# Query phase of a cross-attention kernel: four PSUM banks, one-instruction aggregates for the moments, the first two products split by term, and a new order of work on ScalarE and VectorE

## The chip, the cores and the metric

The kernel runs on one core of a Trainium2 chip. The number that counts is the device time of one execution in microseconds. The kernel before took 1082.04 us (median of 3 runs, 1081.27 to 1082.4). A core has TensorE (PE in the rows), VectorE (DVE), ScalarE (ACT), GpSimd (POOL) and SyncE (SP), which here issues all the DMAs. Each engine works through its own list of instructions in order; semaphores tie the lists together.

## The reference

```
x  : 32 x 100 x 256     ctx : 32 x 361 x 256     16 heads of 64
x  = x + xattn(layernorm(x), ctx, ctx, WQ, WK, WV, WO, mask)
x  = x + ffn(layernorm(x), W1, b1, W2, b2)

xattn: Qh = Q WQ, Kh = K WK, Vh = V WV, softmax(Qh Kh^T / 8 - 1e9 mask) Vh, heads side by side, times WO
ffn:   activations and weights rounded to 8 bits (one scale per tensor), 256 -> 1024, gelu, 1024 -> 256
```

Here mask has the shape 100 x 361 and everything is float32.

## The kernel before

Float32 products are made out of float16 ones. An operand is split into a high float16 part and a low one (the rest), and `split3` adds up three matmuls: high x high, high x low, low x high. In the rows these are lines L368, L369 and L370.

The program has four stages.

1. The query phase, 0 to 98 us. It normalises x and multiplies it by WQ for all 32 batches, while the four attention weights are scaled and split.
2. The turns of the batches. For each batch, K, V, the scores, the softmax, the product with V and the product with WO follow a table of times that gives each engine its order. The table is not changed.
3. The feed-forward network.
4. The output.

The query phase goes in eight chunks of four batches, 400 tokens each. A chunk c takes these steps:

- `stats_x` (VectorE, BN_STATS, one instruction a batch) gives the moments of the even and the odd elements. `ln_moments` joins them in eight small dependent steps, for chunk 0 on VectorE and for the others on GpSimd; GpSimd then makes `rstd` and `shift`.
- `norm_x` (ScalarE, four instructions) writes the normalised `xn`. `x_transposes` (TensorE, eight) brings it into two PSUM banks. `x_high` (ScalarE, two) and `x_low` (VectorE, two) split it into `xnT_h` and `xnT_l`.
- In `q_chunk` TensorE makes eight products m = 0 to 7, each with six matmuls of 400 columns (two halves of the contraction, three terms). They go in turn into PSUM banks `proj[0]` and `proj[1]`. `q_out` copies each product out: ScalarE the even ones, VectorE the odd ones. The semaphores `s_qe` keep product m from starting before product m-2 has been copied. At m = 4 TensorE does the transposes of chunk c+1.

The weights take part in between. `abs_w` (VectorE, two per weight) finds the largest value in each partition, `top_w` (TensorE) transposes it, and `unit_w` (VectorE, three small steps) makes the scale. `high_w` (ScalarE) and `low_w` (VectorE) then write the two parts, half a weight at a time. No product of queries can start before WQ has been through this.

After the last chunk `phase1_over` makes every engine wait for all query outputs. TensorE also waits for GpSimd's memsets (`s_zero`) there, and then begins with the K products, which use the same two banks as the query products.

## Time and profile before

| | us |
|---|---|
| median of 3 runs | 1082.04 |
| the profiled execution | 1081.73 |
| its span | 1079.9 |
| query phase, first to last product | 20.07 to 97.9 |
| PE busy | 1019.1 (94%) |
| DVE busy | 937.4 (87%) |
| ACT busy | 862.5 (80%) |
| POOL busy | 766.1 (71%) |

The span is the time from the first to the last instruction on the core, and 1.8 us of the execution lie around it. In the rows below, a line number such as L368 is the line of the kernel that issued the instruction. Matmuls are pipelined, so one matmul's duration overlaps the next; what a matmul costs in a stream is the distance between two starts. `x4` at the end of a row counts instructions that were merged. `[0.79 <-issue]` is idle time before the instruction and what ended it.

### The profile page before, as it was taken

To read this page: it belongs to the slowest core of one execution; us is meant where nothing else is said; L and a number is where in the kernel's file an instruction comes from. 1 tells how busy PE (TensorE), PEld (TensorE's weight loads), DVE (VectorE), ACT (ScalarE), POOL (GpSimd) and SP (SyncE) were. 2 spreads that over 40 slices of the span, in tenths; PEclk is the share of its full clock that TensorE was granted. 3 is DMA by queue.
4 is the path that set the end of the run, shared out by engine and by line. 5 is a ranking of instruction groups with operands and counts; after the bars stand their busy time and mean duration, and the time that the engine had idled before them with its cause. 6 is when DMAs were issued, how large, how long until landed. Compare 5 with 4: busy or idle time off the path is not lost.

```text
span 1079.9 us, 37623 instructions
## 1 busy us (share of the span) xinstructions
PE 1019.1 (94%) x10639; PEld 650.5 (60%) x10639; DVE 937.4 (87%) x2668; ACT 862.5 (80%) x1809; POOL 766.1 (71%) x1106
## 2 busy tenths in 40 slices
PE   3999999999999999999999999999999999997738
PEld 1555566666666666666666666666666666665327
DVE  5776888888898888888888888888888888886997
ACT  3664888888888888888888888888888888886906
POOL 3336778877777887777887778777777777774700
PEclk9999999999999999999999999999999999999969
DMA  8500676666767676666667767666766666673003
GB/s 238 142 1 14 122 141 139 138 138 138 138 138 140 140 140 139 138 138 138 138 139 140 140 136 138 140 138 139 138 138 139 133 137 140 138 144 127 1 0 123
DMA packets 435437, 136.77 MB, mean 127 GB/s; under 512 B 407666, under 2 KB 434390, under 8 KB 435414
## 3 DMA queue, kind: packets, MB, share of 16 engines
q1 hardware_dynamic: 435414, 136.47, 61.1%
q8 instruction: 13, 0.21, 0.1%
q14 instruction: 10, 0.08, 0.0%
HBM read 28.60 MB, written 6.55 MB: 33 GB/s over the span
## 4 chain that ended last, share of the span: by engine, by line
PE 88%; DVE 7%; ACT 2%; issue 1%; DMA 1%; POOL 0%; ACTq 0%; DVEq 0%; SPq 0%; POOLq 0%
PE front L368 21%; PE front L369 19%; PE front L370 19%; PE back L1309 13%; PE front L1287 7%; PE tp L1287 5%; DVE hrange L1138 3%; DVE hrange L1139 3%; DMA xs<-x 1%; PE front L1424 1%; ACT xn L691 1%; PE tp L1424 1%; PE back L1424 0%; PE front L1192 0%; PE front L1213 0%
## 5 line engine op out<-in xcount | busy, mean ns | idle before, releaser
L616 POOL TENSOR_TENSOR hl<-prob,hl 100x361 f16<-100x361 f32 x511 | 428.6, 853 | 74.6 <-ACT hl L748 73.8
L742 ACT ACTIVATE prob<-prob,nmax 100x361 f32<-100x361 f32 x512 | 295.4, 589 | 5.0 <-DVE nmax L985 3.7
L1309 PEld LDWEIGHTS back<-v,pT 128*128 128x128 f16 (+1 forms) x4608 | 167.8, 98 | 32.3 <-issue 9.6
L748 ACT ACTIVATE hl<-prob 100x361 f16<-100x361 f32 x352 | 175.2, 498 | 3.4
L1309 PE MATMUL back<-v,pT 128*128 128x65 f16 (+1 forms) x4608 | 176.9, 193 | 0.8 <-DMA pT<-hl 0.8
L752 ACT ACTIVATE k_h<-front 128x362 f16<-128x362 f32 x256 | 120.5, 471 | 61.8 <-PE front L370 54.2
L368 PE MATMUL front<-ctx_h,wk_h 128*128 128x362 f16 x512 | 164.0, 320 | 2.4 <-DVE v L1045 1.0
L370 PE MATMUL front<-ctx_h,wk_l 128*128 128x362 f16 x512 | 161.7, 316 | 0.0
L369 PE MATMUL front<-ctx_l,wk_h 128*128 128x362 f16 x512 | 161.4, 315 | 0.0
L1045 DVE SCALAR_TENSOR_TENSOR v<-front,v 128x512 f16<-128x512 f32 (+1 forms) x192 | 132.6, 691 | 30.6 <-ACT v L756 29.9
L756 ACT ACTIVATE v<-front 128x512 f16<-128x512 f32 (+1 forms) x192 | 114.4, 596 | 55.4 <-PE front L370 49.8
L985 DVE CUSTOM_DVE_ANT_0 prob<-tp,mask_g,ngain 100x361 f32<-100x361 f32 x256 | 148.2, 588 | 11.0 <-POOL hl L616 7.6
L985 DVE CUSTOM_DVE_ANT_0 prob<-front,mask_g,ngain 100x361 f32<-100x361 f32 x256 | 148.5, 589 | 5.7 <-POOL hl L616 0.3
L368 PE MATMUL front<-wv_h,ctx_h 128*128 128x512 f16 (+1 forms) x384 | 147.6, 384 | 1.7 <-DVE k_l L1039 1.2
L369 PE MATMUL front<-wv_l,ctx_h 128*128 128x512 f16 (+1 forms) x384 | 145.5, 379 | 0.0
L370 PE MATMUL front<-wv_h,ctx_l 128*128 128x512 f16 (+1 forms) x384 | 145.5, 379 | 0.0
L1039 DVE SCALAR_TENSOR_TENSOR k_l<-front,k_h 128x362 f16<-128x362 f32 x256 | 135.6, 530 | 7.0 <-ACT k_h L752 3.7
L620 POOL TENSOR_TENSOR ahl<-att,ahl 100x256 f16<-100x256 f32 x127 | 85.1, 670 | 36.8 <-ACT ahl L762 36.8
L605 POOL TENSOR_TENSOR ctx_l<-ctx_raw,ctx_h 128x361 f16<-128x361 f32 x64 | 53.2, 854 | 44.3 <-ACT ctx_h L792 44.3
L992 DVE TENSOR_SCALAR_CACHE_REDUCE hl<-prob 100x361 f16<-100x361 f32 x160 | 83.8, 524 | 0.7 <-ACT prob L742 0.6
L368 PEld LDWEIGHTS front<-ctx_h,wk_h 128*128 128x128 f16 x512 | 49.7, 97 | 47.4 <-issue 10.7
L368 PEld LDWEIGHTS front<-wv_h,ctx_h 128*128 128x128 f16 (+1 forms) x384 | 41.1, 107 | 59.2 <-issue 19.1
(206 smaller groups left out, 2047.4 us busy)
## 6 DMA issues: line engine op xcount, KB each, us to landing
ctx_raw<-ctxT SPq DMA_DIRECT2D x33, 361.0 KB, 3.2
pT<-hl SPq DMA_TRANSPOSE x253, 3.6
xs<-x SPq DMA_DIRECT2D x8, 400.0 KB
q_all<-x SPq DMA_DIRECT2D x32, 100.0 KB
out<-q_all SPq DMA_DIRECT2D x32, 100.0 KB
xb<-out SPq DMA_DIRECT2D x5, 640.0 KB, 8.2
out<-xb SPq DMA_DIRECT2D x25, 128.0 KB, 1.8
q_all<-wq SPq DMA_DIRECT2D x1, 1024.0 KB, 6.8
```

Of the source, the lines that this page charges most:

```text
L368: eng.matmul(dst, lh, rh, start=first, stop=False)
L369: eng.matmul(dst, lh, rl, start=False, stop=False)
L370: return eng.matmul(dst, ll, rh, start=False, stop=final)
L616: pool.tensor_tensor(hl[0:T, n % RT, 1, 0:S], prob[0:T, n % RP, 0:S], hl[0:T, n % RT, 0, 0:S], ALU.subtract).then_inc(s_lo, 1)
L742: act.activation(prob[0:T, n % RP, 0:S], prob[0:T, n % RP, 0:S], ACT.Exp, bias=nmax[0:T, n:n + 1], scale=-1.0).then_inc(s_exp, 1)
L748: act.activation(hl[0:T, h % RT, 0, 0:S], prob[0:T, h % RP, 0:S], ACT.Copy).then_inc(s_ha, 1)
L752: act.activation(k_h[:, n % 4, :], ps[:, 0:SE], ACT.Copy, scale=KS).then_inc(s_kh, 1)
L985: dve.tensor_tensor_reduce(prob[0:T, n % RP, 0:S], ring[n % RP][0:T, 0:S], mask_g[0:T, 0:S], ngain[0:T, 0:1], 3.0e38, ALU.add, ALU.min, nm ...
L1039: dve.scalar_tensor_tensor(out=k_l[:, n % 4, :], in0=ps[:, 0:SE], scalar=KS, in1=k_h[:, n % 4, :], op0=ALU.mult, op1=ALU.subtract).then_in ...
L1045: dve.scalar_tensor_tensor(out=v[:, 1], in0=ps[0:rows_of(n), :].rearrange("p (h d) -> p h d", h=HT), scalar=VS, in1=v[:, 0], op0=ALU.mult, ...
L1287: ins = pe.matmul(ring[(2 * n + h) % RP][:, 0:SE], qs[rows[h], n, :], ks[rows[h], n % 4, :], start=t == 0, stop=t == 2)
L1309: ins = pe.matmul(obank[j % 2][:, n % GH * DV:(n % GH + 1) * DV], pT[0:r, n % RT, part_ * ST + st, :], v2[half][0:r, st, v, n % HT, :], st ...
```

## The change

It touches the query phase and the first waits behind it.

- Query products use four banks in turn, `qbank = proj + obank`. Product m waits for the copy of product m-4. ScalarE still takes the even products and VectorE the odd ones.
- TensorE runs small matmuls on the identity from the start: `warm_up(120)` gives 240 matmuls of 64 x 100, half of them into PSUM partitions 0 to 63 and half into 64 to 127. After that come `top_w(0)` and then `x_transposes(0, 0)`, in the other order than before, and 56 more such matmuls.
- `first_two` makes products 0 and 1 of chunk 0 term by term: first all high x high matmuls, then those with `xnT_l`, then those with `wq_l`. The first half of WQ is split in two quarters, so products 0 and 1 need only the first quarter.
- For chunks 0 and 1 the moments come from BN_AGGR, one for each batch, in `pair_x` on VectorE. Two small steps make `var` and `mean` from its output.
- VectorE looks for the maxima of WQ ahead of the statistics of chunk 1, of which one batch goes before `unit_w(0)` and three behind it.
- On ScalarE `norm_x` of a chunk is done in two halves, ahead of and behind `q_out(6)`. The second `high_w` of a chunk moves ahead of `x_high`. In chunk 0 the transposes stand at m = 6 and `norm_x(1)` inside the chunk.
- `phase1_over` and the wait for `s_zero` go from TensorE's list. The first two K products wait for their own bank instead, and the wait for `s_zero` stands before the first scores.

TensorE's list at the start, before. `ident,xn` are the transposes of x and `ident,wabs` is `top_w(0)`.

```order
L1192 MATMUL front<-ident,xn 128x100 x8
L1200 MATMUL tp<-ident,wabs 128x128 x2
L368 MATMUL front<-xnT_h,wq_h 128x400
L369 MATMUL front<-xnT_l,wq_h 128x400
L370 MATMUL front<-xnT_h,wq_l 128x400
```

And now:

```order
L1289 MATMUL tp<-identb 64x100 x240
L1223 MATMUL tp<-ident,wabs 128x128 x2
L1215 MATMUL front<-ident,xn 128x100 x8
L1289 MATMUL tp<-identb 64x100 x56
L1244 MATMUL front<-xnT_h,wq_h 128x400 x4
L1249 MATMUL front<-xnT_l,wq_h 128x400 x4
L1254 MATMUL front<-xnT_h,wq_l 128x400 x4
L370 MATMUL back<-xnT_h,wq_h 128x400
```

In front of everything stand 240 matmuls; `top_w(0)` has moved ahead of the transposes, and the low part of WQ is wanted last in the first two products.

VectorE's list at the start, before. `wabs` are the maxima of WQ, `wtop` to `winv` its scale.

```order
L882 BN_STATS stats<-xs 100x6 x4
L467 TENSOR_TENSOR lnt<-stats 100x4
...
L474 TENSOR_TENSOR var<-lnt 100x4
L882 BN_STATS stats<-xs 100x6 x4
L845 TENSOR_REDUCE wabs<-q_all 128x1 x2
L851 TENSOR_REDUCE wtop<-tp 128x1
L853 TENSOR_SCALAR wunit<-wtop 128x1
L855 RECIPROCAL winv<-wunit 128x1
L875 SCALAR_TENSOR_TENSOR wq_l<-q_all,winv,wq_h 128x2x512
L887 TENSOR_TENSOR xnT_l<-front,xnT_h 128x400 x2
```

And now:

```order
L893 BN_STATS stats<-xs 100x6 x4
L970 BN_AGGR pair<-stats 100x2 x4
L972 TENSOR_SCALAR var<-pair 100x4
L973 TENSOR_SCALAR mean<-pair 100x4
L856 TENSOR_REDUCE wabs<-q_all 128x1 x2
L893 BN_STATS stats<-xs 100x6
L862 TENSOR_REDUCE wtop<-tp 128x1
...
L893 BN_STATS stats<-xs 100x6 x3
L898 TENSOR_TENSOR xnT_l<-front,xnT_h 128x400 x2
L886 SCALAR_TENSOR_TENSOR wq_l<-q_all,winv,wq_h 128x2x256
L970 BN_AGGR pair<-stats 100x2 x4
```

The maxima now precede the statistics of chunk 1; `xnT_l` precedes the low part of WQ, which comes as a quarter.

ScalarE's list in chunk 2, before; the first row holds the last output of chunk 1 and the first of chunk 2.

```order
L703 ACTIVATE q_all<-front 128x4x100 x2
L683 ACTIVATE wk_h<-q_all,winv 128x2x512
L703 ACTIVATE q_all<-front 128x4x100
L699 ACTIVATE xnT_h<-front 128x400 x2
L703 ACTIVATE q_all<-front 128x4x100
L691 ACTIVATE xn<-xs,shift,rstd 100x256 x4
L683 ACTIVATE wk_h<-q_all,winv 128x2x512
```

And now, from the first output of chunk 2:

```order
L708 ACTIVATE q_all<-front 128x4x100
L687 ACTIVATE wk_h<-q_all,winv 128x2x512
L708 ACTIVATE q_all<-back 128x4x100
L687 ACTIVATE wk_h<-q_all,winv 128x2x512
L704 ACTIVATE xnT_h<-front 128x400 x2
L708 ACTIVATE q_all<-front 128x4x100
L695 ACTIVATE xn<-xs,shift,rstd 100x256 x2
L708 ACTIVATE q_all<-back 128x4x100
L695 ACTIVATE xn<-xs,shift,rstd 100x256 x2
```

The block of four `xn` and one `wk_h` between two outputs has been taken apart. The diff, cut to its core:

```
...
     var = place("var", [P, B], F32)
+    pair = place("pair", [P, 2 * TB, 2], F32)
     rstd = place("rstd", [P, B], F32)
...
     obank = [back[:, n * 512:(n + 1) * 512] for n in range(2)]
+    qbank = proj + obank
     obanks = bank + obank + [t[:, :] for t in tp]
...
             w = w if len(w.shape) == 3 else w.rearrange("p (c n) -> p c n", c=KD)
+            if n == 0 and half != 1:
+                return w[:, :, 0:2 * P] if half == 0 else w[:, :, 2 * P:HD // 2]
             return w[:, :, half * HD // 2:(half + 1) * HD // 2]
...
             bs = slice(c * TB, (c + 1) * TB)
-            if c == 0:
-                pool.wait_ge(s_lv, 8)
+            if c < 2:
+                pool.wait_ge(s_lv, (TB + 2) * (c + 1))
             else:
...
-        def norm_x(c, par):
+        def norm_x(c, par, items=range(TB)):
...
             act.wait_ge(s_rs, c + 1)
-            for i in range(TB):
+            for i in items:
                 b = c * TB + i
...
                                      bias=shift[0:T, b:b + 1])
-            ins.then_inc(s_xn, 1)
+            if items[-1] == TB - 1:
+                ins.then_inc(s_xn, 1)
...
             act.wait_ge(s_qp, NM * c + m + 1)
-            act.activation(q_slot[:, c * TB:(c + 1) * TB, m, :], proj[0][:, 0:TW].rearrange("p (b t) -> p b t", b=TB),
+            act.activation(q_slot[:, c * TB:(c + 1) * TB, m, :], qbank[m % 4][:, 0:TW].rearrange("p (b t) -> p b t", b=TB),
                            ACT.Copy, scale=QS).then_inc(s_qe[0], 1)
...
             q_out(c, 2)
+            if c == 0:
+                norm_x(1, 1)
+                q_out(c, 4)
+            if split:
+                high_w(split, 1)
             if more:
                 x_high(c + 1, 1 - par)
-            q_out(c, 4)
+            if c > 0:
+                q_out(c, 4)
             if c + 2 < NB:
-                norm_x(c + 2, par)
+                norm_x(c + 2, par, range(TB // 2))
             if c == NB - 2:
...
                 act.activation(mask_b[0:T, 0:S], mask_b[0:T, 0:S], ACT.Copy, scale=-1.0e9).then_inc(s_mb, 1)
-            if split:
-                high_w(split, 1)
             q_out(c, 6)
+            if c + 2 < NB:
+                norm_x(c + 2, par, range(TB // 2, TB))
         norm_x(0, 0)
...
         high_w(0, 0)
+        high_w(0, 2)
         high_w(0, 1)
-        norm_x(1, 1)
         for c in range(NB - 1):
             if c == NB - 2:
-                act.wait_ge(s_wlo, 8)
+                act.wait_ge(s_wlo, 9)
             q_chunk(c, c % 2)
...
             hi, lo = (part_w(w, n, half) for w in ((wq_h, wq_l), (wk_h, wk_l), (wv_h, wv_l), (wo_h, wo_l))[n])
-            dve.wait_ge(s_whi, 2 * n + half + 1)
+            dve.wait_ge(s_whi, 2 * n + half + 2 if n else (1, 3, 2)[half])
             dve.scalar_tensor_tensor(out=lo, in0=part_w(raws[n], n, half), scalar=winv[:, n:n + 1], in1=hi,
...
-        def stats_x(c):
+        def stats_x(c, items=slice(None)):
...
             dve.wait_ge(s_x[c], 16)
-            for b in range(c * TB, (c + 1) * TB):
+            for b in range(c * TB, (c + 1) * TB)[items]:
                 dve.bn_stats(stats[0:T, b, :], xs[0:T, b, :]).then_inc(s_st, 1)
...
             dve.tensor_scalar(q_slot[:, c * TB:(c + 1) * TB, m, :],
-                              proj[1][:, 0:TW].rearrange("p (b t) -> p b t", b=TB),
+                              qbank[m % 4][:, 0:TW].rearrange("p (b t) -> p b t", b=TB),
                               QS, None, ALU.mult).then_inc(s_qe[1], 1)
...
             q_out(c, 1)
+            if c == 0:
+                low_w(0, 1)
+                stats_x(2)
             if c < 3:
...
                                          op0=ALU.mult, op1=ALU.mult).then_inc(s_wc, 1)
+        def pair_x(c):
+            bs = slice(c * TB, (c + 1) * TB)
+            dve.wait_ge(s_st, TB * (c + 1))
+            for b in range(c * TB, (c + 1) * TB):
+                dve.bn_aggr(pair[0:T, b, :], stats[0:T, b, :]).then_inc(s_lv, 1)
+            dve.wait_ge(s_lv, (TB + 2) * c + TB)
+            dve.tensor_scalar(var[0:T, bs], pair[0:T, bs, 1], EPS, None, ALU.add).then_inc(s_lv, 1)
+            dve.tensor_scalar(mean[0:T, bs], pair[0:T, bs, 0], -1.0, None, ALU.mult).then_inc(s_lv, 1)
         stats_x(0)
-        dve.wait_ge(s_st, TB)
-        ln_moments(chain(dve, s_lv), dve, 0)
-        stats_x(1)
+        pair_x(0)
         abs_w(0, 0)
         abs_w(0, 1)
+        stats_x(1, slice(0, 1))
         unit_w(0)
-        low_w(0, 0)
+        stats_x(1, slice(1, TB))
         start(dve, (s_k, s_v, s_cm, s_cr, s_sv, s_max, s_mg, s_hv, s_ri, s_nrm, s_x1, s_ln))
         x_low(0, 0)
-        low_w(0, 1)
-        stats_x(2)
+        low_w(0, 0)
+        pair_x(1)
+        low_w(0, 2)
         for c in range(NB):
             if c == NB - 2:
-                dve.wait_ge(s_wlo, 8)
+                dve.wait_ge(s_wlo, 9)
             q_chunk(c, c % 2, 2 - max(0, c - NB + 3))
...
+        def first_two():
+            pe.wait_ge(s_whi, 1)
+            for k in range(KD):
+                pe.wait_ge(s_xth, k + 1)
+                for m in range(2):
+                    pe.matmul(qbank[m][:, 0:TW], wq_h[:, k, m * P:(m + 1) * P], xnT_h[:, 0, k, :],
+                              start=k == 0, stop=False)
+            for k in range(KD):
+                wait(pe, s_xtl, k + 1)
+                for m in range(2):
+                    pe.matmul(qbank[m][:, 0:TW], wq_h[:, k, m * P:(m + 1) * P], xnT_l[:, 0, k, :],
+                              start=False, stop=False)
+            pe.wait_ge(s_wlo, 1)
+            for m in range(2):
+                for k in range(KD):
+                    ins = pe.matmul(qbank[m][:, 0:TW], wq_l[:, k, m * P:(m + 1) * P], xnT_h[:, 0, k, :],
+                                    start=False, stop=k == KD - 1)
+                ins.then_inc(s_qp, 1)
         def q_chunk(c, par, more=True):
-            wait(pe, s_xtl, KD * (c + 1))
+            if c == 0:
+                first_two()
+            else:
+                wait(pe, s_xtl, KD * (c + 1))
             for m in range(NM):
-                if m == NM // 2 and more:
+                if m == (6 if c == 0 else NM // 2) and more:
                     x_transposes(c + 1, 1 - par)
...
                     top_f()
-                wait(pe, s_qe[m % 2], NM // 2 * c + m // 2)
-                if c == 0 and m % (NM // 2) == 0:
-                    pe.wait_ge(s_wlo, m // (NM // 2) + 1)
+                if c == 0 and m < 2:
+                    continue
+                if c == 0 and m == 2:
+                    pe.wait_ge(s_wlo, 2)
+                if c == 0 and m == NM // 2:
+                    pe.wait_ge(s_wlo, 3)
+                if c > 0 or m >= 4:
+                    wait(pe, s_qe[m % 2], NM // 2 * c + m // 2 - 1)
                 for k in range(KD):
                     ms = slice(m * P, (m + 1) * P)
-                    ins = split3(pe, proj[m % 2][:, 0:TW], (wq_h[:, k, ms], wq_l[:, k, ms]),
+                    ins = split3(pe, qbank[m % 4][:, 0:TW], (wq_h[:, k, ms], wq_l[:, k, ms]),
                                  (xnT_h[:, par, k, :], xnT_l[:, par, k, :]), k == 0, k == KD - 1)
                 ins.then_inc(s_qp, 1)
+        def warm_up(times):
+            for _ in range(times):
+                for h in range(2):
+                    pe.matmul(tp[1][h * DK:(h + 1) * DK, 0:T], identb[:, h * DK:(h + 1) * DK], identb[:, 0:T],
+                              start=True, stop=True)
+        warm_up(120)
+        top_w(0)
         x_transposes(0, 0)
-        top_w(0)
+        warm_up(28)
         for c in range(NB):
...
-
-        phase1_over(pe)
-        wait(pe, s_zero, PADS)
...
                     g = jobs.index((kind, n, later))
+                    if part == "first" and g < 2:
+                        wait(pe, s_qe[g], NB * NM // 2 - 1)
                     if g >= 2 or part != "first":
...
                 elif kind == "QP":
+                    if part == "first" and n == 0:
+                        wait(pe, s_zero, PADS)
                     if n % (NP_ // 2) == 0:
...
```

## Rows read from the trace of the kernel before

**Rows 1.** Chain of work, start of the program: start, us, what

```profile
12.70 2.26 DVE wabs L845 x2
...
15.01 0.70 PE tp L1200 x2
...
16.58 1.16 ACT wq_h L683
...
18.96 1.06 DVE xnT_l L887 x2
```

**Rows 2.** Waits of PE, 11 to 105 us: us in total, times, longest

```profile
PE front L1192 <- ACT xn L691: 12.1, 1, 12.1
PE front L368 <- DVE xnT_l L887: 4.4, 1, 4.4
PE front L368 <- ACT q_all L703: 3.3, 4, 1.0
```

**Rows 3.** Timeline of PE: start us, us, instruction, count; idle before

```profile
24.04 0.54 PE L368 MATMUL front<-xnT_h,wq_h 128*128 128x400 f16 x1
24.37 0.54 PE L369 MATMUL front<-xnT_l,wq_h 128*128 128x400 f16 x1
...
25.09 0.33 PE L369 MATMUL front<-xnT_l,wq_h 128*128 128x400 f16 x1
25.26 0.33 PE L370 MATMUL front<-xnT_h,wq_l 128*128 128x400 f16 x1
...
26.44 0.85 PE L1192 MATMUL front<-ident,xn 100*128 100x100 f32 x8
27.13 0.33 PE L368 MATMUL front<-xnT_h,wq_h 128*128 128x400 f16 x1
...
31.34 0.33 PE L368 MATMUL front<-xnT_h,wq_h 128*128 128x400 f16 x1
...
93.42 0.60 PE L1208 MATMUL tp<-ident,fabs 128*128 128x128 f32 x4
93.86 0.33 PE L368 MATMUL front<-xnT_h,wq_h 128*128 128x400 f16 x1
...
97.75 0.33 PE L370 MATMUL front<-xnT_h,wq_l 128*128 128x400 f16 x1
98.86 0.31 PE L368 MATMUL front<-ctx_h,wk_h 128*128 128x362 f16 x1 [0.79 <-issue]
...
103.29 0.33 PE L1287 MATMUL front<-k_h,q_h 64*128 64x362 f16 x2
103.45 0.32 PE L1287 MATMUL front<-k_l,q_h 64*128 64x362 f16 x2
```

**Rows 4.** Engines, 20:22: busy (x) of five, then PEclk, DMA share, GB/s

```profile
20.00:22.00 2.00, 1.93 (x6) 0.89 (x7) 2.00 (x5) 0.73 (x2) 0.00 (x0) 1.00 0.65 243
```

**Rows 5.** Chain of work, 46 to 51.5 us

```profile
47.35 1.96 ACT xn L691 x4
49.30 1.04 ACT wk_h L683
50.34 0.40 ACT q_all L703
```

**Rows 6.** Timeline of SP, VectorE and GpSimd at places named in the text

```profile
1.21 0.44 SPq L483 DMA_DIRECT2D q_all<-wq  x1
...
8.30 0.16 DVE L474 TENSOR_TENSOR var<-lnt 100x4 f32<-100x4 f32 x1
...
11.30 1.41 DVE L882 BATCH_NORM_STATS2 stats<-xs 100x6 f32<-100x256 f32 x4 [2.83 <-DMA xs<-x]
...
17.76 1.28 DVE L875 SCALAR_TENSOR_TENSOR wq_l<-q_all,winv,wq_h 128x1024 f16<-128x1024 f32 x1 [1.22 <-ACT wq_h L683]
...
107.00 0.88 POOL L616 TENSOR_TENSOR hl<-prob,hl 100x361 f16<-100x361 f32 x1 [4.18 <-ACT hl L748]
```

**Rows 7.** DMA issues of the page: KB each, median us to landing

```profile
q_all<-wq SPq DMA_DIRECT2D x1, 1024.0 KB, 6.8
```

## Prediction

> **What bounds the kernel now.** I read the chain of work at the start first, then TensorE's waits up to 105 us, then its timeline, since the change ends at the first K product. TensorE is busy 94% of the span, so whatever lets it reach the turns of the batches sooner comes off the end, as long as no other engine then holds it there.
>
> The start is one chain of waits [rows 1, 6]. VectorE sits idle for 2.83 us until x of chunk 1 lands, does its statistics at 11.30, only then the maxima of WQ (12.70, 2.26 us), TensorE transposes them at 15.01, and ScalarE writes the high part of WQ from 16.58. The low part and `xnT_l` (from 18.96) come last, and TensorE has waited 4.4 us when it begins at 20.07 [rows 1, 2]. It then begins slowly. A 400-column matmul starts 0.33 us after the one before it up to 24.37, and 0.17 us after it from 25.09 on [rows 3]. By length these are the two levels of the clock, 1.2 and 2.4 GHz (400 / 2.4 = 167 ns). The granted-clock column reads 1.00 in the slow stretch as well [rows 4], so the level has to be read from the distance between starts. TensorE had done only ten transposes before.
>
> Inside the phase I compare a sum with the clock on the wall. Chunk 1 starts at 31.34 and the last product is over at 97.75 + 0.17 = 97.92, so 66.58 us. The work in it is 7 x 48 = 336 matmuls at 0.169, 56.8 us; six blocks of eight transposes at 27.13 - 26.44 = 0.69, 4.1 us; and eleven small transposes at (93.86 - 93.42) / 4 = 0.11, 1.2 us [rows 3]. That is 62.1, and 4.4 us are stalls. TensorE's row for ScalarE's outputs has 3.3 of them, in four waits of up to 1.0 [rows 2]; the restart behind a wait adds to the rest. The chain names the cause: between two outputs ScalarE does four `xn` (1.96) and one half weight (1.04) before the 0.40 of the output [rows 5], 3.4 us, where two banks give it one product, 6 x 0.169 = 1.01 us. Last, the first K product starts at 98.86, 0.94 us after the products end, behind `phase1_over` [rows 3].
>
> **The change, part by part.** *Start, VectorE.* WQ is issued at 1.21 to 1.65 and takes 6.8 us to land [rows 6, 7], so it is there by about 8.4. The statistics of chunk 0 end at 6.9 (the eight moments steps end at 8.30 + 0.16 [rows 6], and are 0.2 each). The maxima can run from 8.4 to 10.75, hidden in what is today a wait for x. Then comes one statistics instruction at 11.30 (the landing of x, unchanged, 0.4) and at 11.7 the scale, 0.87 as today between 15.71 and 16.58 [rows 1]: ready at 12.55 instead of 16.55.
>
> BN_AGGR is in no row. From above it costs what a BN_STATS does, 1.41 / 4 = 0.35; from below less than half of a moments step, 0.08. I take 0.17, near the moments step, as it too reads a handful of elements. So `pair_x` is 4 x 0.17 and two steps, 1.0 us, against 1.6; its ends are 0.6 and 1.8. In chunk 0 this is beside the path. In chunk 1 it stands on it and can cost 0.8 or give 0.4.
>
> *Start, TensorE.* Today it waits for the normalised x until 12.1 [rows 2]; `pair_x` is 0.6 shorter than the steps it replaces, so the transposes start at 11.5, and last 0.7 at the fast clock. ScalarE splits until 12.95, then makes the first quarter of WQ: a half takes 1.04 [rows 5], a quarter about 0.55. First product at 13.6. VectorE meanwhile: three statistics to 13.65, `xnT_l` (two, 1.06) to 14.8 (with 0.1 allowed for the semaphore increments in front), the low quarter (half of 1.28 [rows 6]) to 15.5, `pair_x(1)` to 16.5, the second low quarter to 17.15. The first twelve matmuls (2.0 us) fit into 13.6 to 16.2, and product 2 starts at 17.2. From there nothing waits: 36 matmuls (6.1), the transposes (0.7), so chunk 1 starts at 24.0. Its inputs are in time: ScalarE does `norm_x(1)` from 18.7 to 20.7 and the transposes stand at 21.2; the low second half of WQ is done by 18.9, product 4 stands at 19.2. These margins are 0.3 to 0.5 us. First term: 31.34 - 24.0 = 7.3 us.
>
> *Chunks.* With four banks an engine has three products, 3.05 us, from the end of its own until its bank is wanted. The longest ScalarE block is now two `xn` (0.98) or one half weight (1.04) plus an output and, in chunk 0, a short wait for GpSimd's moments of chunk 2; VectorE's longest is statistics and scale, 1.4 + 0.9 = 2.3, plus an output. Per chunk of 8.8 us ScalarE has four outputs at 0.4, two `x_high` (two outputs' worth, 0.8 to 1), `xn` at 1.96 and two half weights at 1.04, 6.6 us in all, so it doesn't become the bound. All 4.4 us go. What is late next is nothing within 0.3 us, so TensorE's own 62.1 us bound the phase: 24.0 + 62.1 = 86.1.
>
> *End.* The first K product needs banks 0 and 1, copied during products 5 to 7, so it follows directly: 0.9 us. GpSimd's work on ctx hangs on VectorE's chunk 5 and moves with it. Behind it GpSimd stands idle 4.18 us before its first `hl` [rows 6], enough for what comes. Everything later moves as a block.
>
> *Filler.* This is the one cost that can reach the path. It starts at 2.1. `top_w(0)` waits behind it, and with one statistics instruction in VectorE's way at 11.30 the filler may end at up to 11.3 for nothing. At the slow clock 100 columns take a quarter of 0.333, 0.083 us; at the fast one 0.042. If the clock rises after 4.7 us of streaming, as it did from 20.07 to 24.8, it depends on whether the two halves of a pair overlap. The nearest rows are the scores: two matmuls on halves of the array's rows start 103.29, the next two at 103.45, 0.16 us for 2 x 362 columns, which one after the other would take 0.30 [rows 3]. Halves of its columns are in no row. Overlapping: 56 pairs slow (4.7), 64 pairs at 0.042 (2.7), end at 9.5. One by one: 28 pairs slow (4.7), 92 at 0.084 (7.7), end at 14.5. I take the first, as the rows are nearest to it. The Trainium skill (TensorEngine Tiling, Tiling Modes) says that column tiles too work independently, but its section on restrictions says that column tiling switches the fast weight load off. No run here shows either; the sum stays at 9.5 by the first, and by the second lies between the two ends.
>
> Sum: 7.3 + 4.4 + 0.9 = 12.6 us off 1081.73, 1069.1; the profiled execution is 0.3 below the median of the runs, so 1069.4 against 1082.04.
>
> **Rivals.**
>
> *The filler is late.* Nothing overlaps, it ends at 14.5, and scale, transposes and first product come 3.2 us later. Gain 9.4, time 1072.6. For it: no row shows halves of columns. Against: the rows of the scores.
>
> *The clock is low again at the first products.* The 14 slow matmuls of today (20.07 to 24.8) cost 14 x 0.165 = 2.3 us [rows 3]; while TensorE waits for VectorE anyway, up to 17.2, they cost nothing, and transposes and filler at half rate cost 0.5 to 1. Price 1 to 3 us, gain 9.6 to 11.6, time about 1071.5. What TensorE does between filler and products is ten transposes and waits; today ten transposes before 20.07 did not raise the clock. The Trainium skill (TensorE: Matmul & The Clock Gate, PE-mode transpose) says that transposes don't count as activity for the clock, with which the slow start behind them agrees. By that rule the fast clock would have to last from the filler over the transposes.
>
> *Stalls move instead of going.* If one of the 0.3 us margins in chunk 0 fails or BN_AGGR costs 0.35, or ScalarE's block comes out longer than three products in chunks 2 to 4, 1 to 4 us of stalls stay: 1070.5 to 1073.5.
>
> *Slower than before.* One mechanism: filler matmuls run one at a time and never raise the clock, so that TensorE's list is blocked. The end of the filler may be 11.3 for nothing, and the 12.6 us are used up at 23.9, which is (23.9 - 2.1) / 240 = 0.091 us each. At the slow clock without overlap they take 0.083 and the filler ends at 22.0; with 2.3 us of slow products behind it, that gives 12.6 - 10.7 - 2.3, or 0.4 us slower, 1082.4. Against it: streaming did raise the clock at 24.8.
>
> *It doesn't do what it says.* The phase gets shorter, but the turns of the batches wait for something with its own time, such as DMA. GpSimd would be the first to look at, and its 4.18 us of idle time ahead of the first `hl` [rows 6] speak against it. If they are used up, what is past them is lost: with all 12.6 us taken off TensorE and GpSimd not moving at all, 4.2 would be kept, 1077.8.
>
> **Numbers.** Forecast as worked out 0.62, with a range of its own of 1068 to 1070.4; late filler 0.13; low clock 0.10; stalls that stay 0.10; something else ahead of the turns 0.03; slower 0.02. The range goes from 1067.6 (BN_AGGR cheap, restarts all gone) to 1073.0, which takes in the late filler and most of the stalls. A difference below 0.2%, 2.2 us, can't be told from none; all cases but the last are far above it. Faster 0.97, same 0.01, slower 0.02.
>
> **What would show it.** In the profile after: filler over before 11.3; scale of WQ ready at 12.5; first product near 13.6 with starts 0.17 apart; product 2 at about 17.2; chunk 1 at 24.0; then no wait of TensorE for outputs up to the first K product at 86.1, with 0.17 before it. Starts 0.33 apart behind 13.6 would be the low clock, `top_w(0)` after 14 the late filler, and waits for `q_all` the stalls that stay. If all this is so and the time is still above 1073, the step from the first K product to the end is wrong.

## The result, and the profile after

The changed kernel takes 1069.44 us (median of 4 runs, 1068.56 to 1071.12); the kernel before took 1082.22 beside it. The ratio is 0.9885, with a 95% interval from 0.9868 to 0.9902. The profiled execution took 1068.56 with a span of 1066.7, 13.3 us less than the span before (13.26 ahead of rounding). The forecast was 1069.4, in a range from 1067.6 to 1073.0. The median agrees to the tenth, partly by errors that cancel, as shown below.

TensorE's waits in the changed kernel up to 95 us, in all, times and longest, are the answer to [rows 2]:

```profile
PE tp L1289 <- POOL identb L563: 2.0, 1, 2.0
PE tp L1289 <- issue: 0.9, 1, 0.9
PE front L370 <- DVE k_l L1062: 0.5, 1, 0.5
PE back L370 <- DVE wq_l L886: 0.4, 1, 0.4
PE front L1215 <- ACT xn L695: 0.2, 1, 0.2
```

Not one wait for `q_all` is left. New is the second row: the filler stopped for 0.9 us, and no semaphore ended that. In the rows of the changed kernel the three matmuls of `split3` are lines L370 (high x high), L371 and L372; the fourth row is product 2 of chunk 0, and the third belongs to the turns of the batches. TensorE's timeline at both ends of the query phase, to be held against [rows 3]:

```profile
2.03 6.82 PE L1289 MATMUL tp<-identb 128*64 128x100 f16 x220 [2.03 <-POOL identb L563]
9.75 0.63 PE L1289 MATMUL tp<-identb 128*64 128x100 f16 x20 [0.90 <-issue]
10.37 0.43 PE L1223 MATMUL tp<-ident,wabs 128*128 128x128 f32 x2
10.95 0.91 PE L1215 MATMUL front<-ident,xn 100*128 100x100 f32 x8 [0.15 <-ACT xn L695]
11.79 1.43 PE L1289 MATMUL tp<-identb 128*64 128x100 f16 x56
13.14 0.85 PE L1244 MATMUL front<-xnT_h,wq_h 128*128 128x400 f16 x4
...
15.81 0.34 PE L370 MATMUL back<-xnT_h,wq_h 128*128 128x400 f16 x1 [0.37 <-DVE wq_l L886]
...
22.60 0.33 PE L370 MATMUL front<-xnT_h,wq_h 128*128 128x400 f16 x1
...
84.61 0.33 PE L372 MATMUL back<-xnT_h,wq_l 128*128 128x400 f16 x1
84.78 0.32 PE L370 MATMUL front<-ctx_h,wk_h 128*128 128x362 f16 x1
```

The first product starts at 13.14 instead of 20.07, chunk 1 at 22.60 instead of 31.34, and the first K product at 84.78 instead of 98.86, right behind the last query product. From chunk 1 on the phase takes 84.78 - 22.60 = 62.2 us; its matmuls and transposes alone were worked out at 62.1.

VectorE's part of the chain at the start of the changed kernel, beside [rows 1]:

```profile
1.70 8.97 DMA xs<-x
10.69 0.43 DVE stats L893
...
12.81 1.06 DVE xnT_l L898 x2
13.87 0.66 DVE wq_l L886
14.53 0.30 DVE pair L970 x4
...
15.10 0.67 DVE wq_l L886
15.81 0.34 PE back L370
```

x of chunk 1 landed at 10.69 in this execution, 0.6 sooner than before, and everything from there to product 2 is VectorE's own list. In the other ten profiles with the new start it landed between about 10.1 and 11.3, so a difference of 0.6 lies within the scatter. The other path that could have held the batches back did not: GpSimd's first `hl` stands 8.14 us behind the first K product before and after the change, and its idle time ahead of it went from 4.18 to 3.22 us.

### The profile page after: what moved, and what is told of

Its sections match the earlier page's. It is cut to its first block, busy times and chain, and to the rows that moved or that the text cites. A ratio compares the mean times of both kernels' runs of the same rounds, so it can differ in the third digit from the quotient of the medians.

```text
span 1066.7 us, 38212 instructions
## 1 busy us (share of the span) xinstructions
PE 1022.7 (96%) x10935; PEld 657.5 (62%) x10935; DVE 935.2 (88%) x2673; ACT 860.5 (81%) x1810; POOL 768.2 (72%) x1098
## 4 chain that ended last, share of the span: by engine, by line
PE 89%; DVE 7%; issue 1%; DMA 1%; ACT 1%; POOL 0%; ACTq 0%; DVEq 0%; SPq 0%; POOLq 0%
PE front L370 21%; PE front L372 18%; PE front L371 18%; PE back L1370 13%; PE front L1348 7%; PE tp L1348 5%; DVE hrange L1161 3%; DVE hrange L1162 3%; PE back L370 1%; PE back L372 1%; PE back L371 1%; DMA xs<-x 1%; PE front L1485 1%; PE tp L1485 1%; PE back L1485 0%
## 5 line engine op out<-in xcount | busy, mean ns | idle before, releaser
L370 PE MATMUL front<-ctx_h,wk_h 128*128 128x362 f16 x512 | 164.0, 320 | 1.6 <-DVE v L1068 1.0
L372 PE MATMUL front<-ctx_h,wk_l 128*128 128x362 f16 x512 | 161.7, 316 | 0.0
L371 PE MATMUL front<-ctx_l,wk_h 128*128 128x362 f16 x512 | 161.4, 315 | 0.0
L370 PE MATMUL front<-wv_h,ctx_h 128*128 128x512 f16 (+1 forms) x384 | 147.6, 384 | 1.8 <-DVE k_l L1062 1.2
L371 PE MATMUL front<-wv_l,ctx_h 128*128 128x512 f16 (+1 forms) x384 | 145.5, 379 | 0.0
L372 PE MATMUL front<-wv_h,ctx_l 128*128 128x512 f16 (+1 forms) x384 | 145.5, 379 | 0.0
L370 PEld LDWEIGHTS front<-ctx_h,wk_h 128*128 128x128 f16 x512 | 49.7, 97 | 46.7 <-POOL ctx_l L609 9.8
L370 PEld LDWEIGHTS front<-wv_h,ctx_h 128*128 128x128 f16 (+1 forms) x384 | 41.1, 107 | 59.3 <-issue 19.1
```

The lines of the kernel that those rows point to most:

```text
L370: eng.matmul(dst, lh, rh, start=first, stop=False)
L371: eng.matmul(dst, lh, rl, start=False, stop=False)
L372: return eng.matmul(dst, ll, rh, start=False, stop=final)
```

## The experiments

In these texts the scale of WQ means the start of VectorE's `winv<-wunit`. I measure each run from there to the first K product as well as by the clock, because x lands earlier or later in each execution, and because in some runs the scale waits for TensorE and not for x. The runs were measured in three groups: no_filler to barrier, banks_only to pool_moments, and the last three. Each ratio is against the kernel before as measured in the same group (medians 1081.40, 1082.39 and 1081.91), so medians of different groups compare only roughly.

| kernel | scale of WQ | first K product | between | median us | ratio (95%) |
|---|---|---|---|---|---|
| before | 16.38 | 98.86 | 82.48 | 1082.22 | |
| changed | 11.66 | 84.78 | 73.12 | 1069.44 | 0.9885 (0.9868-0.9902) |
| no_filler | 11.80 | 86.52 | 74.72 | 1071.58 | 0.9912 (0.9896-0.9929) |
| two_banks | 11.71 | 89.06 | 77.35 | 1075.02 | 0.9944 (0.9928-0.9961) |
| act_order | 11.71 | 84.84 | 73.13 | 1068.56 | 0.9888 (0.9871-0.9904) |
| barrier | 12.15 | 86.21 | 74.06 | 1070.03 | 0.9898 (0.9881-0.9914) |
| banks_only | 16.48 | 93.67 | 77.19 | 1078.39 | 0.9964 (0.995-0.9978) |
| steps | 12.23 | 88.12 | 75.89 | 1071.64 | 0.9903 (0.9886-0.9919) |
| one_half | 15.81 | 89.35 | 73.54 | 1074.17 | 0.9929 (0.9912-0.9945) |
| pool_moments | 14.56 | 87.81 | 73.25 | 1071.48 | 0.9894 (0.9878-0.9911) |
| again (changed) | 12.25 | 86.11 | 73.86 | 1070.31 | 0.989 (0.9873-0.9906) |
| wide_filler | 11.57 | 84.69 | 73.12 | 1068.92 | 0.988 (0.9864-0.9897) |
| wide_pool | 11.87 | 84.63 | 72.76 | 1068.63 | 0.9878 (0.9862-0.9895) |

The first group takes one part of the change away at a time.

**no_filler.**

```
-        warm_up(120)
...
-        warm_up(28)
```

> The changed kernel without any of its 296 filler matmuls; all else stays. Theory (the start was worth 7.3 us, of which the clock is a part): the scale of WQ and the first product keep their place (about 11.8 and 13.2 us), but matmuls of 400 columns start 0.33 us apart for about 4.7 us of streaming, of which those before product 2 (15.8) are partly hidden. First K product 1.5 to 3 us later than 84.8, so 86.3 to 87.8, and the time 1.5 to 3 us more. Rival (the fast clock would come by itself, the filler is worth nothing): first K product within 0.3 us of 84.8. Rival (the filler blocks TensorE's list more than it gives): it moves earlier.

TensorE's timeline in this kernel:

```profile
10.46 0.66 PE L1223 MATMUL tp<-ident,wabs 128*128 128x128 f32 x2 [10.46 <-DVE wabs L856]
...
13.83 1.51 PE L1244 MATMUL front<-xnT_h,wq_h 128*128 128x400 f16 x4 [1.21 <-ACT wq_h L687]
15.13 1.54 PE L1249 MATMUL front<-xnT_l,wq_h 128*128 128x400 f16 x4
16.47 1.25 PE L1254 MATMUL front<-xnT_h,wq_l 128*128 128x400 f16 x4
17.55 0.33 PE L370 MATMUL back<-xnT_h,wq_h 128*128 128x400 f16 x1
```

The first eight matmuls are 0.33 us apart (four in 1.3 us, against four in 0.7), and those from 17.55 on 0.17. So TensorE streams its first products at 1.2 GHz without the filler, product 2 starts at 17.55 instead of 15.81, and the first K product comes 1.74 us later. Of this, 0.69 us is there before the first product starts, at 13.83 and not at 13.14 as expected: the eight transposes are slow as well (1.59 us against 0.91). The total is inside what was expected, though by the median and by the ratio the run is 2 to 3 us slower, which single groups of four runs don't settle. In the profiled executions the filler is worth some 1.7 us, and not the 2.3 us of the slow start before, because part of the slow matmuls falls into time in which TensorE waited for VectorE.

**two_banks.**

```
-    qbank = proj + obank
+    qbank = proj + proj
...
-                if c > 0 or m >= 4:
-                    wait(pe, s_qe[m % 2], NM // 2 * c + m // 2 - 1)
+                if c > 0 or m >= 2:
+                    wait(pe, s_qe[m % 2], NM // 2 * c + m // 2)
...
-                        wait(pe, s_qe[g], NB * NM // 2 - 1)
+                        wait(pe, s_qe[g], NB * NM // 2)
```

> The changed kernel with the query products in two banks in turn again (product m waits for the copy of product m-2), the new order on ScalarE and VectorE kept. Theory (four banks remove the 4.4 us of stalls, with room to spare): stalls come back wherever an engine has more than about 1 us between its outputs. ScalarE's blocks are now two xn (1.0) or one half weight (1.04), VectorE's statistics and scale (2.3) still stand, so I expect 2 to 6 us of stalls and the 0.9 us ahead of the first K product partly back; first K product at 87.5 to 91. Rival (the new order alone removes the stalls, the banks give nothing): below 1 us.

4.2 us of stalls came back (77.35 against 73.12), inside what was expected. All of them are inside the chunks. Ahead of the first K product nothing came back, against the expectation: it starts 0.17 us behind the last query matmul. TensorE's waits for outputs:

```profile
PE front L370 <- DVE q_all L903: 2.2, 2, 1.4
...
PE front L370 <- ACT q_all L708: 0.4, 1, 0.4
```

and one of four smaller ones, 0.28 us each from start to start and too short for that list, in the chain of this kernel:

```profile
41.68 0.57 DVE q_all L903
42.26 1.31 DVE stats L893 x4
43.57 0.34 DVE wtop L862
...
44.28 0.48 DVE q_all L903
44.76 0.05 issue
44.81 0.34 PE front L370
```

With ScalarE's blocks taken apart, it is VectorE's work between its outputs that TensorE mostly waits for when there are two banks; one stall of 0.5 us, at 73.7, is ScalarE's. The two longest stalls, 1.54 and 0.97 us from start to start, are in chunk 0, where the new order gives VectorE the most between its outputs.

**act_order.**

```
-            if split:
-                high_w(split, 1)
...
-                norm_x(c + 2, par, range(TB // 2))
+                norm_x(c + 2, par, range(TB if c > 0 else TB // 2))
...
+            if split:
+                high_w(split, 1)
             q_out(c, 6)
-            if c + 2 < NB:
+            if c == 0:
                 norm_x(c + 2, par, range(TB // 2, TB))
```

> The changed kernel with ScalarE's old order in chunks 1 to 7 (four xn together and the second half weight behind them, ahead of the output of product 6), four banks kept. Theory: the block is 2.0 + 1.04 = 3.0 us, plus the 0.4 of the output, and four banks give 3.05 us from the end of a product until its bank is wanted, so three chunks (2 to 4) stall by 0.2 to 0.6 us each, 0.6 to 1.8 in all. Rival (four banks alone do it, the order is worth nothing): first K product within 0.2 us of 84.8. Rival (the order does most of the 4.4 us): over 3 us.

A miss. The first K product stands at 84.84, and TensorE does not wait for an output at all. ScalarE's timeline in chunk 2 of this kernel shows why:

```profile
37.86 0.50 ACT L708 ACTIVATE q_all<-front 128x400 f32<-128x400 f32 x1 [0.68 <-PE front L372]
38.26 2.06 ACT L695 ACTIVATE xn<-xs,shift,rstd 100x256 f32<-100x256 f32 x4
40.23 1.13 ACT L687 ACTIVATE wk_h<-q_all,winv 128x1024 f16<-128x1024 f32 x1
41.27 0.48 ACT L708 ACTIVATE q_all<-back 128x400 f32<-128x400 f32 x1
```

The block begins behind the output of product 4, two products before the end of product 6, and the bank of product 6 is wanted three products after that end. From the end of product 4 that is 5.1 us, less two outputs of 0.4, so 4.2 us for a block of 3.0. With two banks it is 3.05 less 0.8, 2.2, and the block overran it by 0.8 us, which with the restart makes waits of up to 1.0 us [rows 2]. I had taken the 3.05 us behind the end of product 6 for the whole room. With four banks the run shows no gain from ScalarE's new order in chunks 1 to 7 (73.13 us against 73.12).

**barrier.**

```
         for c in range(NB):
             q_chunk(c, c % 2, c < NB - 1)
+        phase1_over(pe)
+        wait(pe, s_zero, PADS)
```

> The changed kernel with TensorE waiting for all query outputs and for the memsets again, ahead of the first K product. Theory: first K product 0.9 us later (85.7), and all of it reaches the turns of the batches. Rival (what follows waits for ScalarE's and VectorE's own barriers anyway): the K product is later but the first mask_g of ScalarE less than 0.4 us.

```profile
85.10 0.33 PE L372 MATMUL back<-xnT_h,wq_l 128*128 128x400 f16 x1
86.21 0.31 PE L370 MATMUL front<-ctx_h,wk_h 128*128 128x362 f16 x1 [0.79 <-issue]
```

The gap is 1.11 less one matmul, 0.94 us, the same as before the change. From the first K product to the first `mask_g` it is 3.98 us with the barrier and without, so all of the 0.94 reaches the batches. By the column from scale to K it is 74.06 against 73.12, the same 0.94.

**banks_only** puts the four banks alone into the kernel before.

```
+    qbank = proj + obank
...
-            act.activation(q_slot[:, c * TB:(c + 1) * TB, m, :], proj[0][:, 0:TW].rearrange("p (b t) -> p b t", b=TB),
+            act.activation(q_slot[:, c * TB:(c + 1) * TB, m, :], qbank[m % 4][:, 0:TW].rearrange("p (b t) -> p b t", b=TB),
...
-                wait(pe, s_qe[m % 2], NM // 2 * c + m // 2)
+                if c > 0 or m >= 4:
+                    wait(pe, s_qe[m % 2], NM // 2 * c + m // 2 - 1)
...
```

> The kernel before with one edit: the query products use four banks in turn, no other part of the change. Theory, as the run with ScalarE's old order left it (banks alone remove the 4.4 us of stalls inside chunks): from the first product to the first K product 78.8 us now become 74.2 to 74.6, no wait for q_all up to the barrier, the 0.94 ahead of K stays; time 4.0 to 4.6 us less. Rival (some stalls are due to the old start or the old order and stay): 1 us or more of waits for q_all left.

From first product to first K product it is 73.51 us against 78.79, 5.28 less, a little more than expected, and no wait for `q_all` is left. The rest is the clock: here nine distances at the start are slow ones, before there were fourteen, and five at 0.165 us are 0.8. So the banks are worth 4.4 to 4.5 us, all the stalls that there were, with the old order on every engine. The median is 4.0 us below that of the kernel before in the same group, as expected.

**steps** goes back to the eight moments steps.

```
-                pool.wait_ge(s_lv, (TB + 2) * (c + 1))
+                pool.wait_ge(s_lv, 8 * (c + 1))
...
-            for b in range(c * TB, (c + 1) * TB):
-                dve.bn_aggr(pair[0:T, b, :], stats[0:T, b, :]).then_inc(s_lv, 1)
...
+            ln_moments(lv_link, dve, c)
```

> The changed kernel with the eight moments steps on VectorE for chunks 0 and 1, in the place of the aggregates. Theory: only chunk 1 stands on the path; the steps take 1.6 us against the 0.56 of four BN_AGGR and two steps, so product 2 and the first K product move by 1.0 us. Rival (what the path waits for is x landing, and the aggregates give nothing): under 0.2 us. Rival (also chunk 0 counts, since WQ's maxima wait behind it): 1.6 us or more.

The steps of chunk 1 took 1.6 us in VectorE's list as expected, 15.53 to 17.13. But the first K product came 2.8 us later than in the changed kernel, measured from the scale of WQ, and not 1.0. The cause is in TensorE's timeline of this run:

```profile
9.75 0.63 PE L1287 MATMUL tp<-identb 128*64 128x100 f16 x20 [1.50 <-issue]
10.95 0.43 PE L1221 MATMUL tp<-ident,wabs 128*128 128x128 f32 x2 [0.57 <-DVE wabs L856]
12.08 1.59 PE L1213 MATMUL front<-ident,xn 100*128 100x100 f32 x8 [0.70 <-ACT xn L695]
13.61 2.54 PE L1287 MATMUL tp<-identb 128*64 128x100 f16 x56
...
19.15 0.33 PE L370 MATMUL back<-xnT_h,wq_h 128*128 128x400 f16 x1
```

The gap in the filler is 1.50 us here, and two more waits follow it, 0.57 us for the maxima of WQ and 0.70 for `xn`; both are later by the longer steps of chunk 0. Then the clock is low again: eight transposes in 1.59 us, against 0.91, and 56 filler matmuls in 2.54, against 1.43. This is the prediction's rival of the low clock, and it came true in this execution. Product 2 starts at 19.15, 1.2 us after VectorE is through with the second quarter of the low part (17.13 + 0.78), and TensorE does not wait for it. So in this run TensorE's slow stretch was the path and VectorE's list was not, and what the aggregates save on the path it does not show.

**one_half** gives both filler matmuls of a pair the same columns of the array.

```
-                    pe.matmul(tp[1][h * DK:(h + 1) * DK, 0:T], identb[:, h * DK:(h + 1) * DK], identb[:, 0:T],
+                    pe.matmul(tp[1][0:DK, 0:T], identb[:, 0:DK], identb[:, 0:T],
```

> The changed kernel with both filler matmuls of a pair on the same 64 columns of the array and the same PSUM partitions, as many as before. Theory (the two halves overlap today, here they can't): the filler takes 0.083 us each at the slow and 0.042 at the fast clock and ends at 14 to 15 instead of 10.4; all behind it is later and the first K product comes 3.5 to 4.5 us later. Rival (the rate is set by issue, not by the array): filler ends at 10.4 again and nothing moves.

```profile
2.03 12.74 PE L1289 MATMUL tp<-identb 128*64 128x100 f16 x240 [2.03 <-POOL identb L563]
```

The filler ends at 14.8, and the first K product comes 4.6 us later, just past the expected 3.5 to 4.5. So the late filler would have been real, and the two halves do overlap in the changed kernel: 220 matmuls in 6.82 us, 31 ns each, against 53 ns here. The profile lists no wait in this filler, which was the first hint at the gap's cause: as many instructions, but 53 ns and not 31 for each.

**pool_moments** puts chunk 1's moments back on GpSimd.

```
-            if c < 2:
+            if c < 1:
...
-        pair_x(1)
```

> The changed kernel with chunk 1's moments back on GpSimd (eight steps there, none on VectorE); aggregates for chunk 0 alone. Theory (VectorE's list is what product 2 waits for): VectorE's path gets 0.56 us shorter, product 2 and the first K product come 0.5 us sooner, since GpSimd has its 2.3 us of steps done before norm_x(1) wants them at 17. Rival (norm_x(1) becomes late and TensorE waits at the transposes): the gain is given back, or 0.3 us are lost.

This run could not answer its question, and showed another thing.

```profile
7.80 0.74 PE L1288 MATMUL tp<-identb 128*64 128x100 f16 x26
12.22 1.04 PE L1288 MATMUL tp<-identb 128*64 128x100 f16 x20 [3.67 <-issue]
```

A gap of 3.67 us, ahead of the last 20 filler matmuls as in the other runs. The edit does not touch TensorE's list up to there. The scale of WQ then comes at 14.56 (VectorE waits 3.06 us for `top_w(0)`). In the profile's list of DMA queues, the instruction queue has a packet in 7 to 8 us in the changed kernel, with a gap of 0.90 that ends at 9.75:

```profile
q8 instruction: 1, 0.02, 6.8%
```

and in pool_moments none in 7 to 8, but one in 9 to 10 us, with the gap ending at 12.22:

```profile
q8 instruction: 1, 0.02, 7.6%
```

In both kernels TensorE goes on 2 to 3 us behind that packet. This pointed to the filler's list running out of instructions, and the last three runs test it.

**again, wide_filler, wide_pool.** The first is the changed kernel. The second is:

```
-            for _ in range(times):
-                for h in range(2):
-                    pe.matmul(tp[1][h * DK:(h + 1) * DK, 0:T], identb[:, h * DK:(h + 1) * DK], identb[:, 0:T],
-                              start=True, stop=True)
+            for _ in range(times):
+                pe.matmul(tp[1][:, 0:2 * P], identb[:, :], ident[:, :].bitcast(F16), start=True, stop=True)
...
-        warm_up(120)
+        warm_up(56)
...
-        warm_up(28)
+        warm_up(12)
```

and the third has this and the edit of pool_moments.

> The changed kernel itself, as the yardstick for the two others of this call. In all profiles with the 240 small filler matmuls the last 20 wait for nothing that the profile shows, 0.4 to 3.7 us, and a packet of the instruction queue ends shortly before they go on (in the changed kernel in 7 to 8 us, in the run with 3.7 us in 9 to 10). Theory: the filler's list (a load and a matmul each) is used up faster than instructions arrive beside the loads of x and WQ, so the gap and with it the time scatter: first K product between 84.5 and 88. Rival: the gap of 0.9 comes back as it was.

> The changed kernel with wide filler: 56 and 12 matmuls of 128 x 256 columns in the place of 240 and 56 of 64 x 100, so 136 instructions for 592 and about the same time on the array (18 at 0.213, 38 at 0.107 us, end near 10.1). Theory (instructions arrive too late for the small filler): no gap in the filler, scale of WQ ready as soon as x of chunk 1 and the maxima allow (11.7 to 12.2), first K product 84.3 to 85.3, and a time as the best runs of the changed kernel or up to 1 us below its median. Rival (the gap has nothing to do with the number of instructions): a gap of 0.4 to 3.7 us ahead of top_w(0) again.

> wide_filler and chunk 1's moments on GpSimd as in pool_moments. In pool_moments the gap of 3.7 us in the filler hid what the edit does. Theory (VectorE's list is what product 2 waits for): first K product 0.4 to 0.6 us sooner than in wide_filler, measured from the scale of WQ on. Rival (norm_x(1) gets late): TensorE waits at the transposes of chunk 1 and the gain is given back.

The changed kernel once more:

```profile
2.03 6.58 PE L1289 MATMUL tp<-identb 128*64 128x100 f16 x220 [2.03 <-POOL identb L563]
10.57 0.63 PE L1289 MATMUL tp<-identb 128*64 128x100 f16 x20 [1.96 <-issue]
...
12.18 2.55 PE L1289 MATMUL tp<-identb 128*64 128x100 f16 x56
```

and wide_filler:

```profile
2.03 7.73 PE L1288 MATMUL tp<-ident,identb 128*128 128x256 f16 x56 [2.03 <-POOL identb L563]
10.08 0.43 PE L1223 MATMUL tp<-ident,wabs 128*128 128x128 f32 x2 [0.31 <-DVE wabs L856]
```

The same kernel that had a gap of 0.90 has one of 1.96, the clock is low again behind it (56 filler matmuls in 2.55 us), and its first K product is at 86.11 instead of 84.78. Of these 1.33 us, 0.59 is the scale of WQ, for which VectorE now waits for TensorE, and 0.74 is the slow stretch. With fewer and wider filler matmuls there is no gap, the clock is up (four matmuls of the first products in 0.7 us from 12.78), and TensorE waits for VectorE's maxima as it should. In the eight profiles with 240 small filler matmuls the profile lists a gap of 0.4 to 3.7 us in seven, always behind matmul 220, and none in one_half; with wide filler there was none in either profile.

The traces say more about where the gap ends. In the changed kernel, barrier and steps matmul 220 started at 8.64, 9.15 and 8.04, and in all three TensorE went on at 9.75. So the end of the gap does not depend on when TensorE gets there. In all seven it comes 2.3 to 2.8 us after the start of the packet in the instruction queue. In one_half the packet starts at 10.92 and matmul 221 at 13.72, 2.8 us later; its predecessor starts at 13.55, so the slow filler reached the place just as the instructions did, and 0.13 us of gap is there too. That the small filler outruns its instructions is what fits all of this, and wide_filler is the test of it by an edit. That their fetch stands in line behind the loads of x and WQ is not shown: no run took the loads away.

wide_pool answers the question of pool_moments: 72.76 us from the scale to the first K product against 73.12, 0.36 less, a little short of the expected 0.4 to 0.6. Product 2 starts at 15.48 with no wait, 3.61 us behind the scale against 4.15 in wide_filler, so VectorE's list had held it; 0.12 us of the gain is given back at the transposes of chunk 1.

As times, the two wide kernels (1068.92 and 1068.63) stand 1.4 and 1.7 us below the changed kernel measured beside them (1070.31), and the intervals of the ratios overlap. What their two traces show is a start without the gap and the low clock; what the median gains is not settled to better than a microsecond. Of the versions run, wide_pool has the lowest ratio, by less than the intervals can tell.

## Why the prediction was right

**The start was sized 7.3 us and gave 8.7.** Chunk 1 starts at 22.60 and not at 24.0. Of the 1.4 us, 0.6 is x landing at 10.69 in this execution, which was not forecast and lies within the scatter of the other runs. 0.44 is BN_AGGR, which I had in no row and put at 0.17; four of them and the two steps took 14.45 to 15.01 and not 1.0 us. Another 0.1 is the allowance in front of `xnT_l`, which was not needed, and the last 0.2 or so lies spread over the small steps. The order of the path was as told: product 2 waits for the second quarter of the low part, at the end of VectorE's list. That this list is the path, the wait of 0.37 us ahead of product 2 says, and wide_pool shows it (a list shorter by 0.56 us, product 2 earlier by 0.54). What the aggregates save against the old steps is 1.04 us of VectorE's time (0.56 against 1.6); how much of it the path would feel, no run shows, since in steps the clock was low.

**The stalls were sized 4.4 and went whole.** banks_only shows that it is the banks. The prediction left it open how much the new order of ScalarE adds and had its block as a risk; act_order puts it at nothing. The rule for a block is wrong in the prediction's working: the time allowed begins at the engine's last output, not at the end of its next product.

**The end was sized 0.9 and gave 0.94**, by the barrier run. It is the barrier and not the banks: in two_banks too the first K product follows directly.

**The filler was read rightly from the scores' rows and yet ended late.** Its halves overlap, and 220 of the 240 were through at 8.85, ahead of the 9.5 worked out, but the last 20 at 10.38. What I had no row for was that it would stop before its last 20, most likely for want of instructions. In the profiled run that cost nothing, as TensorE had transposed VectorE's maxima by the time that VectorE, held by x until 10.69, wanted them at 11.03; in the run again and in pool_moments the first K product came 1.3 and 3.0 us later than in the profiled run.

The Trainium skill (TensorE: Matmul & The Clock Gate, PE-mode transpose) says that transposes don't count as busy time for the clock in the way that other matmuls do, and that the fast level doesn't engage for them. What the traces show is this. In the changed kernel the eight transposes and the gap of 0.90 left the clock up (56 filler matmuls in 1.43 us), and so did the gap of 1.45 in act_order. With the gap of 1.50 and two waits more in steps, and with the gap of 1.96 in again, it was down. So the rival had its chance for good reason, but among these runs the idle time around the transposes decided it.

**The sum.** The first K product came 14.1 us sooner, not 12.8, and the span is 13.3 us shorter. 0.8 us are lost behind the first K product. The first `mask_g` of ScalarE is 14.08 sooner than before, the third 13.84, the last of the 32 13.66, and the end 13.27. I made no run on these, but the profiles at hand sort two of the steps. From the first to the second `mask_g` it is 25.3 us in the kernel before and in banks_only, and 25.5 in all eleven profiles with the new start; why stays open. From the last `mask_g` to the end it is 132.7 us in five profiles and 133.1 in the eight in which VectorE makes aggregates for both chunks, the changed kernel's among them. The 0.4 us stand at one place in the feed-forward network, which the change does not touch. It is VectorE's second row here, which in the kernel before starts 0.12 us behind the first:

```profile
972.79 0.16 DVE L1045 TENSOR_TENSOR red<-red,row 100x1 f32<-100x1 f32 x1 [1.43 <-ACT row L788]
973.28 0.16 DVE L1047 SCALAR_TENSOR_TENSOR red<-row,red 100x1 f32<-100x1 f32 x1 [0.34 <-issue]
```

So this loss goes with what stands ahead of it in VectorE's list and not with scatter; its cause is not shown. The median of the runs lies 0.9 above the profiled one and not 0.3; gaps like that of the run again could do that, but the other executions have no trace. So the forecast's 1069.4 was met by a start that was 1.4 us better than told, 0.8 us of losses that were not in the sum, and a profiled execution 0.6 us further below the median than assumed: the mechanism and each term's sign held, and the agreement to a tenth is luck.

## What to carry to other kernels

When an engine hands its bank back late, count the room for a block from the engine's last output to the moment when the next bank is wanted, not from the end of the product in between. By that count two banks were short by about a microsecond and four had one to spare, and then the order of ScalarE's work did not matter. Where filler raises TensorE's clock, try few and wide matmuls first: 240 small ones stopped for want, it seems, of instructions while the loads were under way, and the idle time that followed could undo what the filler was for. And where a run is to test one engine's list, check in its trace that this engine was still the one waited for: in steps it was not.

## What the runs showed of the hardware

- Four BN_AGGR on 100 x 6 in a row take 0.37 to 0.38 us together (changed kernel), less than 0.1 each, against 0.20 from start to start for a dependent moments step.
- Two matmuls on the two column halves of the array overlap. While the clock is low, 30 matmuls of 100 columns start in a microsecond in the changed kernel and 15 in one_half, where both use one half; while it is high, 54 and 27. Over the whole stretch that is 31 ns each against 53. The rise of the clock can be seen in this count, while the granted-clock column (the third figure from the end) stays at 1.00:

```profile
5.00:6.00 1.00, 1.00 (x34) 1.00 1.00 397
6.00:7.00 1.00, 1.00 (x54) 1.00 1.10 378
```

- The clock rose at about 5.8 us in the changed kernel's filler; in the eight profiles with small filler, which began at 2.03 in all, it rose between 4.6 (steps) and 6.9 (barrier). In the kernel before it rose at 24.8 in products that began at 20.07, and in banks_only, with products that began at 20.16, at 23.3. A start at the slow clock is not the same length in each execution.
- TensorE stopped for 0.4 to 3.7 us in a list of 240 small matmuls at the same place, ahead of the last 20, in seven of eight profiles, and went on 2.3 to 2.8 us after a packet of the instruction queue had started.
